# Gated residual over 128 batches: pieces of 64 KB dealt to the DMA engines in turn, and the gate spread to the partitions in that order

## The reference

```
h = silu(q_pool @ W1.T + b1)
gate = sigmoid(h @ W2.T + b2)[:, None, :]
...                      # a, details = Haar levels of v
a = a * gate             # and each dc = dc * gate, then the inverse
...
return v + a             # and outside: x = x + that
```

## Time and profile before

| | us |
|---|---|
| median of 3 runs | 166.78 (166.63 to 167.11) |
| the profiled execution | 166.82 |
| its span, first to last instruction | 165.1 |
| DVE busy | 80.0 (48%) |
| PE busy | 22.7 (14%) |
| moved in all | 69.47 MB, mean 421 GB/s |
| HBM read, written | 35.92 MB, 33.55 MB |

### The profile page before, as it was taken

The page is one execution under the profiler, slowest core; times in us unless marked ns, Lnnn a source line. Parts: engine busy times, 40 slices in busy tenths (PEclk is TensorE's granted clock), DMA queues, the critical chain, the costliest instruction groups (busy, mean ns, idle before and its releaser), DMA issues.

```text
span 165.1 us, 219 instructions
## 1 busy us (share of the span) xinstructions
PE 22.7 (14%) x68; PEld 12.2 (7%) x68; DVE 80.0 (48%) x20; ACT 2.5 (2%) x3; POOL 2.6 (2%) x10
## 2 busy tenths in 40 slices
PE   0099969800000000000000000000000000000000
PEld 0093722300000000000000000000000000000000
DVE  0052380499999999999970000000004999700000
ACT  3000100100000000000000000000000000000000
POOL 6000000000000000000000000000000000000000
PEclk9999987995555555555555555555555555555555
DMA  5999969969998997989997996999899799799995
GB/s 151 474 456 508 476 286 508 508 286 476 508 397 365 508 508 254 508 349 413 508 429 334 508 508 302 461 508 413 349 508 445 334 492 508 318 445 405 445 421 254
DMA packets 1732, 69.47 MB, mean 421 GB/s; under 512 B 194, under 2 KB 194, under 8 KB 324
## 3 DMA queue, kind: packets, MB, share of 16 engines
q1 hardware_dynamic: 1008, 43.25, 61.4%
q10 hardware_dynamic: 724, 26.22, 36.9%
HBM read 35.92 MB, written 33.55 MB: 421 GB/s over the span
## 4 chain that ended last, share of the span: by engine, by line
DMA 50%; DVE 19%; PE 12%; DVEq 5%; ACT 1%; issue 0%
DMA ring<-in_x 23%; DMA out<-ring 22%; DVE ring L242 10%; DVE ring L247 5%; DVEq L30 5%; DMA ring<-in_L_cond_W 5%; PE gate_sum L173 3%; PE turned L181 2%; PE hidden_sum L151 2%; PE turned L135 2%; DVE ring L229 2%; PE hidden_sum L146 1%; PE turned_cond L140 1%; DVE factor L237 0%; DVE ring L222 0%; ACT ring L193 0%
## 5 line engine op out<-in xcount | busy, mean ns | idle before, releaser
L242 DVE TENSOR_TENSOR ring<-ring,factor 128x16384 f32<-128x16384 f32 x3 | 51.5, 17220 | 0.0
L247 DVE TENSOR_TENSOR ring<-ring,factor 128x8192 f32<-128x8192 f32 x2 | 17.3, 8688 | 40.5 <-DMA ring<-in_x 40.5
L216 DVE COPY ring<-turned 128x512 f32<-128x512 f32 x4 | 2.8, 692 | 10.0 <-PE turned L135 10.0
L237 DVE TENSOR_SCALAR factor<-turned 128x512 f32<-128x512 f32 x4 | 2.8, 691 | 6.9 <-PE turned L181 6.9
L173 PE MATMUL gate_sum<-ring 128*128 128x512 f32 x8 | 5.4, 833 | 1.3 <-DVE ring L227 1.3
L135 PE MATMUL turned<-identity,ring 128*128 128x128 f32 x16 | 3.6, 423 | 8.4 <-DMA ring<-in_L_cond_W 8.4
L229 DVE COPY ring<-turned 128x512 f32<-128x512 f32 x4 | 3.9, 1056 | 0.0
L135 PEld LDWEIGHTS turned<-identity,ring 128*128 128x128 f32 x16 | 3.3, 227 | 8.4 <-issue 8.4
L181 PE MATMUL turned<-ring 128*128 128x512 f32 x8 | 3.7, 601 | 0.8 <-ACT ring L193 0.8
L151 PE MATMUL hidden_sum<-ring 128*128 128x512 f32 x8 | 3.7, 605 | 0.0
L222 DVE TENSOR_TENSOR ring<-hidden_sum,ring 128x512 f32<-128x512 f32 x1 | 0.7, 692 | 5.6 <-ACT ring L190 5.6
(11 more groups left out here) (17 smaller groups left out, 6.6 us busy)
## 6 DMA issues: line engine op xcount, KB each, us to landing
out<-ring ACTq DMA_DIRECT2D x2, 4096.0 KB, 20.8
ring<-in_L_cond_W ACTq DMA_DIRECT2D x1, 1024.0 KB, 7.7
ring<-in_L_cond_W SPq DMA_DIRECT2D x1, 1024.0 KB, 7.5
ring<-in_cond SPq DMA_DIRECT2D x1, 256.0 KB, 7.7
ring<-in_x SPq DMA_DIRECT2D x3, 34.6
b_row<-in_L_cond_b ACTq DMA_DIRECT2D x2, 2.0 KB
out<-ring SPq DMA_DIRECT2D x2, 45.6
ring<-in_x ACTq DMA_DIRECT2D x1, 38.6
```

Source lines behind the costliest of these rows:

```text
L216: dve.tensor_copy(w1_t[:, c, :], turned[c][:, :]).then_inc(w1_t_set, 1)
L242: dve.tensor_tensor(ring[:, c, :, :], ring[:, c, :, :], steps_of(c, STEPS), ALU.mult).then_inc(chunk_scaled, 1)
L247: dve.tensor_tensor(ring[:, 0, piece(h), :], ring[:, 0, piece(h), :], steps_of(CHUNKS - 1, PIECE), ALU.mult).then_inc(chunk_scaled, 1)
```

## The change

The DRAM side of each transfer of x and of the output is viewed as 16 by 8 pieces: for e of 16 and a of 8, piece 16a + e of the group. The SBUF side stays 128 partitions, so the transfer's order gives piece 16a + e to partition 8e + a. Partitions 8e to 8e + 7 now hold eight pieces that lie 1 MB apart in DRAM, and the first pieces of the 16 such blocks are neighbours in DRAM. Size and number of pieces, chunks, slots and halves are as before.

The batch of partition p in chunk g is then 32g + 4(p % 8) + (p // 8) // 4. `spread` is built to that order: a memset to zero and, for each group, one affine select that sets a one where batch and partition meet. TensorE waits for all four of them (`spread_set` at `GROUPS`), and multiplies with the same shapes.

```diff
+DMA_ENGINES = 16
...
-    x_parts = x.rearrange("(g q) (h n) d -> g (q h) n d", g=GROUPS, h=GROUPS)
-    out_parts = out.rearrange("(g q) (h n) d -> g (q h) n d", g=GROUPS, h=GROUPS)
+    DEALS = P // DMA_ENGINES
+    PER_DEAL = DMA_ENGINES // GROUPS
+
+    def dealt(t):
+        pieces = t.rearrange("b (h n) d -> (b h) n d", h=GROUPS)
+        return pieces.rearrange("(g a e) n d -> g e a n d", g=GROUPS, e=DMA_ENGINES)
+
+    x_parts, out_parts = dealt(x), dealt(out)
...
-        spread = ring[:, SCRATCH, 22:22 + GROUPS, 0:P]
+        spread_rows = ring[:, SCRATCH, 22:22 + GROUPS, 0:P]
+        spread = spread_rows.rearrange("s g (i h a) -> s g i h a", h=GROUPS, a=DEALS)
...
-            return parts[c // PER_GROUP, :, r * STEPS:(r + 1) * STEPS, :]
+            return parts[c // PER_GROUP, :, :, r * STEPS:(r + 1) * STEPS, :]
...
-            pool.memset(spread, 1.0).then_inc(ones_spread, 1)
-            pool.wait_ge(ones_spread, 1)
-            pool.affine_select(out=spread, in_=spread, compare_op=ALU.is_ge, fill=0.0, base=0,
-                               pattern=[[P, GROUPS], [1, P]], channel_multiplier=-GROUPS).then_inc(lower_set, 1)
-            pool.wait_ge(lower_set, 1)
-            pool.affine_select(out=spread, in_=spread, compare_op=ALU.is_ge, fill=0.0, base=GROUPS - 1,
-                               pattern=[[-P, GROUPS], [-1, P]], channel_multiplier=GROUPS).then_inc(spread_set, 1)
+            pool.memset(spread, 0.0).then_inc(zeros_spread, 1)
+            pool.wait_ge(zeros_spread, 1)
+            for g in range(GROUPS):
+                pool.affine_select(out=spread[:, g, :, :, :], in_=spread[:, g, :, :, :], compare_op=ALU.not_equal, fill=1.0,
+                                   base=g * (B // GROUPS), pattern=[[1, PER_DEAL], [0, GROUPS], [PER_DEAL, DEALS]],
+                                   channel_multiplier=-1).then_inc(spread_set, 1)
...
-            pe.wait_ge(spread_set, 1)
+            pe.wait_ge(spread_set, GROUPS)
...
-                pe.matmul(spread_gate[g][:, :], spread[:, g, :], gate, start=True, stop=True).then_inc(gate_spread, 1)
+                pe.matmul(spread_gate[g][:, :], spread_rows[:, g, :], gate, start=True, stop=True).then_inc(gate_spread, 1)
...
-                act.dma_start(chunk(out_parts, CHUNKS - 1)[:, piece(h), :],
+                act.dma_start(chunk(out_parts, CHUNKS - 1)[:, :, piece(h), :],
```

More of the change, by code:

```diff
@@ L74, in gated_residual_program @@
         hidden_turned, hidden_t_set = sem("hidden_turned"), sem("hidden_t_set")
-        ones_spread, lower_set, spread_set = sem("ones_spread"), sem("lower_set"), sem("spread_set")
+        zeros_spread, spread_set = sem("zeros_spread"), sem("spread_set")
         gate_summed, gate_set = sem("gate_summed"), sem("gate_set")
```

## The result

The changed kernel takes 285.99 us (median of 4 runs, 284.75 to 288.55), the kernel before 166.70 (median of 4): a ratio of 1.717, with a 95% interval of 1.713 to 1.722. Its profiled execution took 284.75 us, with a span of 282.9. The forecast was slower, with 316 us and a range from 205 to 325. So the sign was right, and so was the mechanism that sets the price (two DMA engines at a time on one way into SBUF); the case I held to be likeliest (300 to 325) is not the one that came. Single runs more than 1.5% above the fastest run of their kernel are left out of every ratio in this document.

What follows compares the result with a forecast made beforehand. One gapless line of eight 19.35 us transfers, set by the 16 DMA engines' rate, bounds the kernel. Doubling them adds 154.8 us, giving an execution of 321.6, less 5.6 for the engines' lead: 316 us, range 205 to 325.

Steps and rivals of the forecast that it cites:

- the case I held to be likeliest: Whole execution: full price, every transfer at half rate, 300 to 325 us; chance 0.55.
- What bounds the kernel: Whole execution: one gapless line of eight transfers of 19.35 us, set by the rate of the 16 DMA engines.
- The DRAM side, taken at nothing: Order of the 64 KB pieces in DRAM: bounds 0.9 us less and nothing; nothing was taken.
- The faster rival: Packets keep 2.42 us and chunk 2's late load comes in 19.35 us: 165.9 us; chance 0.06.
- the late transfer: Load of chunk 2, 47.7 to 67.9 us: 20.2 us long, 0.9 us late, kept in the sum.
- The SBUF side, upper end: Entry to SBUF: two engines share one way, a packet takes 4.84 us, a transfer 38.7, adding 154.8 us in all.
- The lead, 5.6 us back: Within engine pairs: one leads by 0.2 to 0.5 us, giving back 0.35 us in each of 16 transfer halves.
- part of the price: Engines sharing ways meet only partly; 283 us if the mixed stretch keeps 38.7 us, case 205 to 300; chance 0.25.
- No difference: Ways to SBUF unshared or wide enough, deciding at over 54 GB/s a way: 166.8 us within 0.5; chance 0.12.

Runs made afterwards that it cites:

- e1: The changed kernel with the DRAM side viewed as 32 by 4 pieces in place of 16 by 8; 166.63 us, ratio 0.9994 to the kernel before.
- e10: Kernel before, plain 128-run form, with pieces 256 KB apart in DRAM and the gate built by a memset and four selects; 167.85 us, ratio 1.0057.
- e7: Kernel before with the store of chunk 0 issued by ACT, not SP, beside the load of chunk 2; 166.99 us, ratio 1.0019.
- e2: Transfers alone, no gate or product: 8 MB load plain 21.8 us, 16 by 8 43.2; 16 by 4 to partitions 0 to 63 22.9, to 32 to 95 12.6.
- e5: Transfers alone: an 8 by 8 load took 43.1 us; with a 4 by 4 load to other partitions ahead of it, both together 34.7 us.
- e8: Changed kernel with SP issuing the store of chunk 1 only when chunk 0 is stored; 299.30 us, ratio 1.790 to the kernel before.
- e9: Kernel before with only the gate's part of the change, a memset and four selects; 166.82 us, ratio 1.0004.

## Why the prediction was right, and where it was not

**What bounds the kernel.** Right. The line of transfers sets the time in both kernels, and its stretches add up to the difference of the spans.

**The DRAM side, taken at nothing.** Right for this order, as e1 shows (0.9994). That any order is free was too much: e10 pays 0.6%. The faster rival, which let the late transfer go by a better order, is refuted by e1 and e7: the late transfer is the first turn from loads to stores. My sum kept its 0.9 us, and there it was wrong: at the turn of the changed kernel the last load packets take 5.08 us like those ahead of them, and the third load costs 39.9 us, not more than the others. This is why it costs only 19.7 us more than before.

**The SBUF side, upper end.** Right in kind, and the choice of the upper end was right: the three loads run at 208 GB/s, with the engines in step from first to last. Slightly off in size: a packet takes 5.04 us and not 4.84, so 40.3 us and not 38.7 a transfer. Two engines on one way together get 4% less than one gets alone; what takes it isn't known.

**The lead, 5.6 us back.** This step failed. I took the engines' lead from the earlier trace rows, where only loads run, and let it stay at 0.2 to 0.5 us in all sixteen halves. Where only loads run it is of that kind, and smaller: of the eight packets of an engine in a load, six take 5.09 us and two 4.91, so a half gives back 0.18 us. From 130 us on it is another matter. Eight transfers at 40.3 would be 322 us; the five behind the loads took 34.1, 87.2 and 30.8, together 152.1, where 5 x 40.3 = 201.5 would have been without any relief: 49 us back, not 5.6.

The trace's packets show where that begins. The first two store packets of every engine, from 128.4 us on, take 2.60 and 2.43 us in the mean, the third 4.70. Those two are 5 of the 6 us by which the store of chunk 0 is shorter than a load. The dealt store that starts on idle engines (L52 of e2) doesn't have them: its first packets take 4.8 to 5.1 us. So it is the turn from loads to stores that sets the pairs free for two packets. That one engine of a pair still writes SBUF while the other already reads it can't be the whole reason, since the sixteen start their stores within 1.4 us of each other. Where each engine has loads and stores in turn, as in the two started together in e2 (L56), the same is seen: its loads take 4.14 us in the mean, its stores 2.70. Why a store packet behind a load packet is let through stays open.

From there on the engines meet less often. They end the store of chunk 0 2.8 us apart, having entered it 1.4 apart, and from 190 to 204 us, with eight engines on loads and eight on stores at any time, a packet takes 2.45 us, nearly the full rate of the kernel before. That distance is worth that much is shown by e5 (43.1 to 34.7 us); e8 agrees, since taking the distance away costs some of the time again. How the 49 us divide between distance and the mixing of loads with stores isn't shown.

**The rivals.** The time fell into the one called part of the price, to which I gave 0.25. Its 283 us, for a mixed stretch that stays at 38.7, comes close by chance: that stretch took 54.9 us, and the store of chunk 0 and the last halves gave the rest. Against that rival I had held that the second slice of a burst shrinks with time; this row of loads alone says nothing of what follows when loads and stores meet. No difference is refuted, and its point of decision is measured: two engines on a way get no more than one engine's rate (5.0 us a packet in L44 of e2, 2.5 in L46).

**The rest.** Chunk 0 landed at 50.1 us (near 48 foretold), DVE's products took 17.2 us, the packets were 1732. The four selects took 0.41 us each where I had 0.29, `spread` was ready at 3.6 us, and e9 gives it no price.

**The map of the ways.** The Trainium skill, SBUF — State Buffer, section "Door 1: The DMA port swizzle", has partitions 32 further on the same port, and that is borne out: L44 and L50 of e2 run at half rate, and with engines on both sides of partition 64 the rate is whole (L46). The same section counts the ports by the partitions that a transfer reaches, all 16 for 128 partitions. By that count the changed kernel's transfers would run at full rate; they ran at 208 GB/s. The measurement decides: what counts is on how many ports the engines stand at one moment, and here that is half of them.

## What to carry to other kernels

The share of partitions that an engine gets matters as much as the number of engines: a transfer over 128 partitions runs at full rate only if its engines stand on different ports at the same time, so when a view of DRAM is rearranged, keep its rows at four SBUF partitions (the 32 by 4 view of e1) or keep the 128 plain runs. If the DMA share is near 1, look at the GB/s and at the time of a packet before calling the engines saturated. Before an order in DRAM is improved, look whether any packet waits for DRAM: here all but sixteen of the 64 KB packets took the same 2.42 us, so there was nothing to win.

## What the runs showed of the hardware that I had not expected

- A load and a store on shared ports cost less together than one after the other: 60.5 us for a dealt load and a dealt store started together, 43.2 and 42.2 alone (e2), and 41 by the engines' own rate (16 packets of 2.42 us and 2.4 of latency). In it the loads took 4.14 us a packet and the stores 2.70; why is open.
- Adding a 1 MB load ahead of a 4 MB one made the two together 8.4 us faster than the second alone (e5).
- Engines that share ports drift apart widely: in e8 the last store's first engine is done 37 us before its last one, in the changed kernel 17 us. The end of the execution then runs with part of the engines idle, a DMA share of 0.68 in the changed kernel's last stretch.
- The first turn from loads to stores costs once, 0.9 us in the kernel before and 0.5 in e1, and not again (e7); in the changed kernel, whose packets are slow anyway, it doesn't show.
